# Two attention stages of a decoder kernel: PSUM banks of the next key and value, one clamp, the first queries and one rounding moved

## What is computed

```
# layer 0, causal attention (computed once, result added to x, then layer norm)
q, k = rope(x @ wq.T), rope(x @ wk.T);  v = x @ wv.T
p = softmax(q @ k.T / sqrt(128) * key_factor, causal)
x = layernorm(x + (p @ v) @ wo.T)
# ... quantised cross attention, stream mixing ...
# layer 1, gated attention
q, k = rope(x @ Wq.T), rope(x @ Wk.T);  v = x @ Wv.T
y = (decay * (q @ k.T)) @ v
y = y * rsqrt(mean(y * y) + 1e-5) * silu(x @ Wg.T)
x = layernorm(x + (y * gnorm_w) @ Wo.T)
# ... cross attention over ctx, then a linear layer with LoRA
```

## Time and profile before

| | |
|---|---|
| median of 3 runs | 1550.76 us (1549.72 to 1556.24) |
| the profiled execution | 1555.24 us, span 1553.3 us, so 1.9 us lie around the span |
| PE busy | 1439.7 us, 93% of the span |
| DVE, ACT, POOL busy | 1080.7, 823.0, 587.0 us |
| causal stage | 0 to 390 us of the span |
| gated stage | 566 to 1022 us of the span |

### The profile page before, as it was taken

How to read it: one execution, slowest core, us unless ns; L and a number is a source line. 1 busy time by engine, 2 the same in 40 slices (tenths; PEclk the granted TensorE clock), 3 DMA queues, 4 the chain that set the end, 5 groups by cost and what they waited for, 6 DMA issues and landing times.

```text
span 1553.3 us, 23538 instructions
## 1 busy us (share of the span) xinstructions
PE 1439.7 (93%) x7314; PEld 1179.8 (76%) x7314; DVE 1080.7 (70%) x2447; ACT 823.0 (53%) x2074; POOL 587.0 (38%) x611
## 2 busy tenths in 40 slices
PE   6999999998899858999999999979999999999977
PEld 5778888886688736777777787767888888888862
DVE  4687767796587967667767766766776676676662
ACT  4657665654221226557646655636566566566430
POOL 4455444431022236556557555424132132232010
PEclk9999999999799969999999999989999999999998
DMA  7011110000323222222221321220111111011000
GB/s 304 1 69 68 69 68 28 40 31 11 140 82 122 97 79 70 96 72 79 95 98 51 122 95 55 110 80 28 47 49 69 39 57 68 29 66 60 1 1 27
DMA packets 30126, 107.65 MB, mean 69 GB/s; under 512 B 3847, under 2 KB 13191, under 8 KB 22104
## 3 DMA queue, kind: packets, MB, share of 16 engines
q1 hardware_dynamic: 30040, 106.58, 18.9%
HBM read 97.07 MB, written 9.50 MB: 69 GB/s over the span
## 4 chain that ended last, share of the span: by engine, by line
PE 56%; issue 17%; DVE 15%; POOL 8%; ACT 3%; DMA 1%; POOLq 0%; SPq 0%; DVEq 0%; ACTq 0%
PE bank L180 11%; PE bank L181 11%; PE bank L182 11%; PE bank L1667 7%; PE bank L1653 3%; PE bank L1611 2%; PE bank L1149 2%; PE bank L279 1%; POOL yss L1330 1%; PE bank L310 1%; POOL tmp L158 1%; DVE tmp L164 1%; POOL q L1323 1%; PE bank L333 1%; DVE q L686 1%
## 5 line engine op out<-in xcount | busy, mean ns | idle before, releaser
L158 POOL TENSOR_TENSOR tmp<-tmp,sin 128x512 f32<-128x512 f32 x80 | 115.4, 1443 | 232.2 <-ACT tmp L151 229.2
L1927 DVE SCALAR_TENSOR_TENSOR logit<-bank,qss,amask 128x512 f32<-128x512 f32 x128 | 91.6, 748 | 88.2 <-PE bank L182 87.9
L182 PE MATMUL bank<-wo_low,att_high 128*128 128x512 f32 x384 | 150.6, 392 | 0.0
L1667 PE MATMUL bank<-probT,v 128*128 128x256 f32 x512 | 124.4, 386 | 1.2 <-ACT probT L1773 1.2
L1849 POOL TENSOR_TENSOR qss<-qss,half 128x4 f32<-128x4 f32 x32 | 34.9, 1091 | 227.6 <-DVE qss L1913 227.6
L180 PE MATMUL bank<-l_wo_high,att_high 128*128 128x512 f32 x256 | 104.7, 409 | 11.8 <-DVE att_low L559 10.6
L1773 ACT ACTIVATE probT<-bank 128x512 f32<-128x512 f32 x128 | 69.6, 595 | 86.9 <-PE bank L1653 86.8
L1764 ACT ACTIVATE prob<-logit,rmax 128x512 f32<-128x512 f32 x128 | 91.5, 716 | 39.2 <-DVE rmax L1931 39.2
L1511 PE MATMUL bank<-kT,wg 128*128 128x256 f32 x512 | 110.9, 379 | 0.7 <-ACT prob L1529 0.7
L1511 PEld LDWEIGHTS bank<-kT,wg 128*128 128x128 f32 x512 | 97.1, 190 | 14.2 <-ACT prob L1529 1.1
L149 ACT ACTIVATE tmp<-bank 128x512 f32<-128x512 f32 x80 | 47.6, 595 | 113.5 <-PE bank L182 110.4
(11 more groups left out here) (260 smaller groups left out, 4154.4 us busy)
## 6 DMA issues: line engine op xcount, KB each, us to landing
wq<-in_l_wq SPq DMA_DIRECT2D x16, 1024.0 KB, 7.0
wo<-in_l_wo SPq DMA_DIRECT2D x16, 1024.0 KB, 4.8
wkv<-in_l_wkv SPq DMA_DIRECT2D x16, 512.0 KB, 5.5
wg<-in_l_wg SPq DMA_DIRECT2D x8, 1024.0 KB, 4.9
wq<-in_x_wq SPq DMA_DIRECT2D x8, 1024.0 KB, 7.2
wo<-in_x_wo SPq DMA_DIRECT2D x8, 1024.0 KB, 4.9
kT<-in_x_wkv SPq DMA_DIRECT2D x8, 512.0 KB, 4.3
kv_keys<-logit SPq DMA_DIRECT2D x8, 512.0 KB, 4.8
```

What stands on the lines that cost most here:

```text
L158: eng.tensor_tensor(halves(tmp[4 + j % 2]), halves(tmp[2 + j % 2]), per_batch(sin), ALU.mult).then_inc(sem(f"{l}_sinp"), 1)
L182: return eng.matmul(dst, a_high, b_low, start=False, stop=stop)
L1667: last = pe.matmul(bank[VALUE_BANKS[s % 2]][:, 0:L], v[at][:, b * CT + kt, :], probT[s % 2][:, kt, :], start=(kt == 0), stop=(kt == CT - 1))
L1927: dve.scalar_tensor_tensor(logit[s % 2][:, c, :], bank[3 + c][:, :], qss[p][:, 1, h, 2 * b + c:2 * b + c + 1], amask[:, c, :], ALU.mult, A ...
```

## The change

1. Gated stage, PE and ACT: the next key goes to bank 1 and waits for `clamp(2)`, the next value to bank 0 and waits for `clamp(3)` (before: key to bank 0 after `clamp(3)`, value to bank 1). Output tiles 2 and 3 go to banks 6 and 7 and lose their own wait. The first value and key of the stage go to banks 4 and 3. Query 0 of a group waits for the key's copies, query 1 for the value's copy (in group 0 neither does; score 1 waits for the value's copy there).
2. Gated stage, DVE: `clamp(3)` ahead of `mean(0)`.
3. Causal stage, group 0: query 2 moves from ahead of the steps into step 0, query 3 from step 0 into step 1, with their copies and rotations; ACT rounds the first query weights ahead of the value's copy; POOL splits the keys of group 1 after the last query's sine part and not after the key's.
4. Causal stage, all groups: the quarters of the next value stand in steps 1 to 4 (before: 2 to 5). In groups 1 to 7 ACT does `headed(-1)` ahead of the copies of the fourth query, and DVE does `rest(-1)` ahead of `maxima(1)`.

```diff
 # l0_tensor, body
+                    if s == 0 and first:
+                        query(0, 0, 2, bank[6], ("l0_v", 1))
+                    if s == 1 and first:
+                        query(0, 0, 3, bank[0], ("l0_unproj", 2))
-                        if 2 <= s <= 5:
-                            value(n, 1 - p, (s - 2,))
+                        if 1 <= s <= 4:
+                            value(n, 1 - p, (s - 1,))
...
-            query(0, 0, 2, bank[6], ("l0_v", 1))
 # l0_scalar, body
+                    if s == 1 and first:
+                        rope_psum_copies(act, "l0", 0, 4, bank[0])
...
-                    if s == 0:
+                    if s == 0 and first:
+                        rope_psum_copies(act, "l0", 0, 3, bank[6])
+                    if s == 0 and not first:
+                        headed(-1)
                         rope_psum_copies(act, "l0", g, 4, bank[0])
...
-            value(0, 0)
             act.wait_ge(sem("l0_wq0"), 16)
             for c in range(KC):
                 act.activation(wq_high[0][:, c, :], wq[0][:, c, :], ACT.Copy).then_inc(sem("high_part"), 1)
-            for j, k in enumerate((1, 0, 1, 6)):
+            value(0, 0)
+            for j, k in enumerate((1, 0, 1)):
 # l0_gpsimd
+                if isinstance(g, int) and g == 0:
+                    rope_sin_part(pool, "l0", 0, 3)
                 rope_sin_part(pool, "l0", g, 4)
+                if isinstance(g, int) and g == 0:
+                    split_keys(1, 1)
...
-            split_keys(1, 1)
 # l0_vector, body
                 for s in range(STEPS):
+                    if s == 1 and not first:
+                        rest(-1)
                     maxima(s)
-                    if s >= 2 or not first:
+                    if s >= 2 or (s == 0 and not first):
                         rest(s - 2)
+                    if first and s < 2:
+                        rope_sum(dve, "l0", 0, s + 2, qT[0][:, s + 1, :])
...
+                    if s == 2 and first:
+                        rope_sum(dve, "l0", 0, 4, qT[0][:, 3, :])
 # l1
-        L1_OUT = [3, 4, 0, 6]
+        L1_OUT = [3, 4, 6, 7]
-                if due(4 * n):
-                    pe.wait_ge(sem("l1_gclamp"), 4 * n)
-                project_split(pe, bank[0][:, :], l1_wk, slice(0, HD), l1_xT, "l1_proj")
+                if due(4 * n - 1):
+                    pe.wait_ge(sem("l1_gclamp"), 4 * n - 1)
+                project_split(pe, dst[:, :], l1_wk, slice(0, HD), l1_xT, "l1_proj")
...
-                    key(n)
-                    value(n, 1 - p, (0, 1))
+                    key(n, bank[1])
+                    value(n, 1 - p, (0, 1), bank[0])
...
+                clamp(3)
                 mean(0)
-                clamp(3)
```

More of the change, by code:

```diff
@@ L464, in body @@
                         value(n, 1 - p)
-                    if s or not first:
+                    if s:
                         headed(s - 1)
@@ L521, in l0_gpsimd @@
             pool.wait_ge(sem("ld_const"), 6 * 16)
-            rope_sin_part(pool, "l0", 0, 0)
-            split_keys(1, 1)
-            for j in range(1, 4):
+            for j in range(3):
                 rope_sin_part(pool, "l0", 0, j)
@@ L587, in body @@
                     normalise(s)
-                    if s < 2:
+                    if s < 2 and not first:
                         rope_sum(dve, "l0", g, s + 3, qT[p][:, s + 2, :])
+                    if s == 2 and first:
+                        rope_sum(dve, "l0", 0, 4, qT[0][:, 3, :])
                     if 4 <= s <= 6 and not last:
```

59 lines of the change are left out of this document (30 added, 29 removed).

## The result

| | before | after |
|---|---|---|
| median, first measurement | 1553.50 us (4 runs) | 1528.78 us (4 runs) |
| median, second measurement | 1553.95 us (9 runs) | 1529.21 us (5 runs) |
| profiled execution, span | 1555.24, 1553.3 us | 1526.58, 1524.6 us |

The ratio is 0.984 (95% interval 0.9804 to 0.9877), and 0.9827 (0.9808 to 0.9847) the second time. Both pairs of medians lie 24.7 us apart. The forecast was 26.2 less, at 1524.6, with a range of 1517 to 1535; the forecast's own range was 1519 to 1530.

The account below looks back on a forecast made before the run. PE, busy for 93% of the span, was taken as the bound, so only its idle time or lower clock could go. Terms 13.0 - 1.25 + 6.1 + 6.2 - 1.2 + 3.3 = 26.2 us off 1550.8 gave 1524.6, range 1517 to 1535.

Parts of the forecast that it names:

- seven gated groups: Gated stage: the key no longer waits for the clamp, 1.85 us gained a group, 13.0 us for seven.
- last gated group: Last gated group: mean(0) now stands behind the clamp, so outputs(1,0) starts later, 1.25 us lost.
- entry: Gated stage entry: query 0 follows the key at once, 3.4 us, and the clock stays up, 2.7 us; together 6.1.
- causal groups 2 to 5: Causal stage: earlier headed(-1) and rest(-1) start out_late sooner, 1.25 us gained a group; DVE's idle time hides later copies.
- groups 1 and 6: Causal groups with quantise: DVE lacks idle time, so 0.6 us of delay is on the path; 1.2 us lost in two.
- first causal group: Causal group 0: scores(0) at 23.3, scores(3) at 39.0, turn(2) following without its wait; 3.3 us gained, bounds 2.0 and 6.
- still find their `normalise` done, by 0.5 us: Causal step 5: turn(5) and turn(6) come 0.9 us earlier without waiting for DVE, so moving the value's quarters costs nothing.
- with the same delay for all behind it: Last gated group: everything after outputs(1,0) was taken to shift by the same 1.25 us.
- A: Rival: clock stays low at the gated entry, 2.7 us, or new low stretches in groups 1 and 6, up to 1.7 each; chance 0.13.
- B: Rival: the causal stage gives nothing, 8.3 us gone and 17.9 left, time 1532.9; chance 0.07.
- C: Rival: POOL holds the gated clamp and the wait moves to outputs(1,1), 4.2 us, time 1528.8; chance 0.10.
- D: Rival: PE without pauses gets the lower clock in the steady gated stage, slower than before, 1577; chance 0.02.

Follow-up runs that it names:

- e4_entry_back: Changed kernel with only the first value and key of the gated stage back in banks 1 and 0; 1536.25 us, 0.9899 of the kernel before.
- e2_causal: Causal stage of the changed kernel with the gated stage of the kernel before; 1543.99 us, 0.9954 of the kernel before.
- e5_mean_first: Changed kernel with mean(0) ahead of clamp(3) again in all gated groups; 1526.01 us, 0.9816 of the kernel before.
- e7_rope_early: Changed kernel with the fourth query's rotation ahead of normalise(2) in causal group 0; 1527.25 us, 0.9825 of the kernel before.

## Why the forecast came out as it did

Going by distances of marks in which no stretch at the lower clock differs, or by the mean where it does:

| term | forecast | measured | from |
|---|---|---|---|
| seven gated groups | 13.0 | 12.2 | 7 x 1.74 |
| last gated group | -1.25 | -1.9 | 66.9 and 68.8 |
| entry | 6.1 | 6.1 | `e4_entry_back` |
| causal groups 2 to 5 | 5.0 | 5.0 | 1.1, 1.3, 1.3, 1.3 |
| causal group 7 | 1.25 | 1.5 | `e2_causal`: 224.2 for 225.7 to the first key, both with 41 us at the lower clock |
| groups 1 and 6 | -1.2 | -0.8 | 47.4 for 47.0, twice |
| first causal group | 3.3 | 0.9 or 2.1 | with and without the stretch on query 2 |
| sum | 26.2 | 23.0 or 24.2 | measured by medians: 24.7 |

**Gated groups: right.** The mechanism is the one given, down to the mean that sits behind POOL. 1.74 and not 1.85: 0.1 a group is what `e5_mean_first` gives back.

**Entry: right**, in both parts, 3.5 of wait for 3.4 and 2.6 of clock for 2.7.

**Causal groups 2 to 7: right.** In group 2 the wait ahead of `out_late` went from 1.92 to 0.81 us, in the others it is nearly gone. Groups 1 and 6 lost by the mechanism given (the copies push `exps(1)` and with it DVE), 0.4 where 0.6 was put. That the quarters cost nothing holds only together with the new order; the step "still find their `normalise` done, by 0.5 us" doesn't hold for groups 1 and 6, in which PE waited 0.6 us ahead of `turn(5)` before as well.

**The last gated group: too small.** The 1.3 us of wait was right. The step that failed is "with the same delay for all behind it": what a pause of 3.2 us in one piece does to the clock behind it wasn't asked. At the entry the same question had been asked and answered.

**The first causal group: the term that was mis-sized.** Two steps failed. First, `scores(0)` was to start at 23.3 and started at 24.05 to 24.9 in twelve profiles: POOL's sine part for the first query took 1.77 us beside DVE's L164 of the same query, where those of later queries took 1.26 to 1.29. With it `scores(3)` came at 39.5 to 40.1 where no early stretch lay, not at 39.0. Second, I counted a low stretch only as something that could go, not as one that comes: behind the 1.9 us ahead of `scores(0)` query 2 ran at the lower clock in five of twelve profiles, which cost 1.5 us and put `scores(3)` at 41.1 to 41.4. The forecast's own bound of 2.0 didn't hold in the kernel's own profile (0.9). And its upper bound, 6 us with no low stretch behind the pause ahead of `scores(3)`, was out of reach as well: `e2_causal` had none and gained 2.3, since DVE sets the start of group 1. The fast rotation alone gave 1.6 more (`e7_rope_early`).

**The base.** 4.2 us of difference remain between 1524.6 and 1528.8. Of these 1.5 are the terms. The other 2.7 are the step "I give the forecast against the median": 1550.8 was the middle of three runs, and over 42 runs of the kernel before the median is 1553.3 us. Against its own execution the sum gave 1529.1, 0.3 from the measured median, but that is luck in part: the profile before had more at the lower clock than most runs.

**Why the profiles differ by 28.7.** 23.0 are the terms. Between the start of group 7 and the first gated key the kernel after has 37.5 us at the lower clock for 41.0, and gains 2.9 where 1.5 are the change: 1.4. Behind the last key it gains 2.3 where the last group loses 1.9: 4.2 that the code doesn't explain, and there the kernel after has 24 us at the lower clock and the one before 31, 3.4 of the difference at the place shown above. At half rate 7 us less are worth at most 3.5, an estimate; the rest stays open. 23.0 + 1.4 + 4.2 = 28.6.

**Rivals.** A fell at the entry but was right in kind elsewhere. New stretches at the lower clock came where I had put them, in group 6 of the first profile and in groups 1 and 6 of the second, but there they cost nothing, not 1.7 us each, since DVE sets the pace. Those that cost time came where I hadn't looked, in the first causal and in the last gated group. B fell with 6.8 us from the causal stage alone. C fell with the clamp's 0.68 us beside POOL and `outputs(1,1)` without a wait. D fell: the granted clock was 1.00 from 592 to 974,

```profile
592.00:974.00 382.00, 375.26 (x1892) 300.91 (x1891) 280.47 (x633) 240.94 (x598) 221.07 (x198) 1.00 0.24 82
```

with PE 98% busy.

## What to carry to other kernels

Price an idle time of PE with the clock behind it, for pauses that a change makes as well as for those that it removes: here pauses of 1.9 to 3.3 us cost up to 2.6 us more. Then ask who sets the pace behind it: where PE would wait for DVE anyway, a stretch at the lower clock cost nothing. Compare kernels by distances between fixed marks of the trace, and runs by span times granted clock; a median of three runs was 2.5 us off as a base, as much as the terms that were in question. Where one engine sets the pace, as DVE in groups 1 and 6, the costs of two edits need not add up (0.8 and 0.5 us alone, 0.4 together): try all four combinations before a cause is named.

## What the hardware showed that was not expected

The clock's price was not the same in each execution of one kernel: with 1.86 to 1.87 us of idle time ahead of `scores(0)`, query 2 ran at the lower clock in some profiles and not in others, though nothing there differs in code or waits. What decides it stays open. The same holds for the 2.1 us ahead of `turn(4)` and, once in ten, for the 3.3 us ahead of `scores(3)`.

DVE's rotation beside POOL: L164 took 1.78 us at 31.76 in the kernel after, with POOL's L158 from 31.70 for 1.29, where 0.69 is its time alone:

```profile
31.76 1.78 DVE L164 TENSOR_TENSOR tmp<-tmp,cos 128x512 f32<-128x512 f32 x1
33.57 0.69 DVE L168 TENSOR_TENSOR qT<-tmp 128x512 f32<-128x512 f32 x1
```

```profile
31.70 1.29 POOL L158 TENSOR_TENSOR tmp<-tmp,sin 128x512 f32<-128x512 f32 x1 [6.08 <-ACT tmp L151]
```

Which of the two gets longer went by which began first in these rows. For the first query DVE began 0.04 us ahead, and POOL's part was the longer one, 1.77 us:

```profile
21.55 0.69 DVE L164 TENSOR_TENSOR tmp<-tmp,cos 128x512 f32<-128x512 f32 x1
```

```profile
21.59 1.77 POOL L158 TENSOR_TENSOR tmp<-tmp,sin 128x512 f32<-128x512 f32 x1 [0.90 <-ACT tmp L151]
```
